# Edge logarithms, first group and first ticks of graph attention beside the projection of linear attention; hidden products and gelu ahead of the gates

## What is computed

```python
xn = _layernorm(x)
x = x + _L0_gnn_ref(xn, ...) + _L0_mix_ref(xn[None], ...)[0]   # GCN + linear attention
x = x + _L0_ffn_ref(_layernorm(x)[None], ...)[0]               # 8 experts of 192, top 2, gelu
xn = _layernorm(x)
x = x + _L1_gnn_ref(xn, ...) + _L1_mix_ref(xn[None], ...)[0]   # graph attention + linear attention
x = x + _L1_ffn_ref(_layernorm(x)[None], ...)[0]               # 8 experts of 3072 + a shared one
```

## Time and profile before

| what | us |
|---|---|
| median of three runs | 2092.32 |
| the profiled execution | 2091.71 |
| its span | 2089.8 |
| TensorE busy in it | 1883.1 |
| VectorE busy | 1306.9 |
| ScalarE busy | 909.6 |
| GpSimd busy | 219.7 |

### The profile page before, as it was taken

How to read it: one execution, slowest core, us unless ns; L and a number is a source line. 1 busy time by engine, 2 the same in 40 slices (tenths; PEclk the granted TensorE clock), 3 DMA queues, 4 the chain that set the end, 5 groups by cost and what they waited for, 6 DMA issues and landing times.

```text
span 2089.8 us, 30875 instructions
## 1 busy us (share of the span) xinstructions
PE 1883.1 (90%) x12246; PEld 1788.8 (86%) x12247; DVE 1306.9 (63%) x2404; ACT 909.6 (44%) x1497; POOL 219.7 (11%) x169
## 2 busy tenths in 40 slices
PE   5988998978997999488757999999999999999998
PEld 4876888977887999488747999999999999999998
DVE  6997766442335544888866575355656666667786
ACT  2331213312222542566733323334555655666776
POOL 0000000003000001565710000000010101000010
PEclk9998999997999999689979999999999999999999
DMA  3110002100111311100022112125565756676895
GB/s 111 46 46 1 24 27 95 54 1 24 69 46 45 106 54 49 64 19 21 16 106 71 53 63 98 69 100 213 190 208 197 234 207 227 245 246 231 284 319 205
DMA packets 36795, 234.29 MB, mean 112 GB/s; under 512 B 5916, under 2 KB 7318, under 8 KB 14632
## 3 DMA queue, kind: packets, MB, share of 16 engines
q1 hardware_dynamic: 31318, 217.41, 29.3%
q0 software_dynamic: 2656, 8.99, 1.9%
q10 hardware_dynamic: 2674, 5.87, 0.7%
HBM read 221.91 MB, written 10.35 MB: 111 GB/s over the span
## 4 chain that ended last, share of the span: by engine, by line
PE 75%; DVE 13%; issue 8%; ACT 2%; DMA 2%; POOL 1%; SPq 0%; DVEq 0%; POOLq 0%; ACTq 0%
PE bank L313 16%; PE bank L315 15%; PE bank L314 15%; PE bank L2441 8%; PE bank L570 4%; PE bank L2442 3%; PE bank L2453 3%; DVE weight_lo L286 2%; PE bank L2457 2%; PE bank L2445 2%; PE bank L2454 2%; PE bank L2456 1%; DVE mix_kv L793 1%; PE bank L2444 1%; DVE gat_unread L2034 1%
## 5 line engine op out<-in xcount | busy, mean ns | idle before, releaser
L286 DVE TENSOR_TENSOR weight_lo<-weight_raw,weight_hi 128x2304 fp32r<-128x2304 f32 (+1 forms) x155 | 389.9, 2519 | 36.7 <-ACT weight_hi L276 36.5
L276 ACT ACTIVATE weight_hi<-weight_raw 128x2304 fp32r<-128x2304 f32 (+1 forms) x155 | 323.3, 2087 | 92.2 <-DMA weight_raw<-in_ffn_w 52.0
L313 PE MATMUL bank<-xT_hi,weight_hi 128*128 128x306 f32 (+1 forms) x576 | 183.8, 319 | 4.0 <-issue 2.0
L314 PE MATMUL bank<-xT_lo,weight_hi 128*128 128x306 f32 (+1 forms) x576 | 178.8, 310 | 0.0
L315 PE MATMUL bank<-xT_hi,weight_lo 128*128 128x306 f32 (+1 forms) x576 | 178.5, 310 | 0.0
L313 PE MATMUL bank<-weight_hi,xT_hi 128*128 128x384 f32 (+1 forms) x480 | 160.2, 334 | 9.3 <-DVE xT_lo L334 4.5
L2815 DVE TENSOR_TENSOR hidden_tmp<-hidden_tmp,bank 128x160 f32<-128x160 f32 (+5 forms) x192 | 65.7, 342 | 160.3 <-ACT hidden_tmp L2601 160.3
L315 PE MATMUL bank<-weight_hi,xT_lo 128*128 128x384 f32 (+1 forms) x480 | 156.8, 327 | 0.0
L314 PE MATMUL bank<-weight_lo,xT_hi 128*128 128x384 f32 (+1 forms) x480 | 156.8, 327 | 0.0
L570 PE MATMUL bank<-one_hot_dst,one_hot_src 125*128 125x313 f16 x800 | 122.8, 305 | 15.2 <-ACT packed_counts L584 7.9
L313 PE MATMUL bank<-weight_hi,hidden_hi 128*128 128x384 f32 (+1 forms) x366 | 124.6, 340 | 0.9 <-DVE weight_lo L286 0.9
(11 more groups left out here) (491 smaller groups left out, 5178.5 us busy)
## 6 DMA issues: line engine op xcount, KB each, us to landing
weight_raw<-in_ffn_w SPq DMA_DIRECT2D x111, 1152.0 KB, 5.2
weight_raw_fifth<-in_ffn_w SPq DMA_DIRECT2D x25, 1152.0 KB, 5.3
weight_raw<-in_shared_w SPq DMA_DIRECT2D x16, 1152.0 KB, 5.2
weight_raw<-in_mix_kv SPq DMA_DIRECT2D x8, 1152.0 KB, 7.1
weight_raw<-in_gat_w SPq DMA_DIRECT2D x8, 768.0 KB, 4.9
weight_raw<-in_mix_q SPq DMA_DIRECT2D x4, 1152.0 KB, 5.1
weight_raw<-in_mix_out SPq DMA_DIRECT2D x4, 1152.0 KB, 5.2
weight_raw<-in_gnn_w SPq DMA_DIRECT2D x4, 1152.0 KB, 5.4
```

The source lines that it names most:

```text
L276: act.activation(upper_, whole_, ACT.Copy).then_inc(*w_hi.one())
L286: dve.tensor_tensor(lower_, whole_, upper_.bitcast(F32), ALU.subtract).then_inc(*w_lo.one())
L313: pe.matmul(dst, a[0], b[0], start=first, stop=False)
L314: pe.matmul(dst, a[0], b[1], start=False, stop=False)
```

## The change

In dense_experts: the logits are made with the gate matrix stationary (8 columns) and 320 tokens moving, 36 matmuls, kept as 8 rows and turned by five transposes. TensorE makes units 0 to 5 of the hidden products around them, then the counts, the gates, unit 6, the seven spread gate rows, and goes on as before from unit 7. gelu goes to `acted`, which holds all units of a half and lies in the place of hT's lower half; the multiply and the lower half are made in place. The weight split that stood behind unit 5 stands ahead of unit 6. The last token tile has 113 columns in the output products, and the pads go.

```diff
+    def logits():
+        pe.wait_ge(*gate_lo.at(1))
+        for s, (a0, n) in enumerate(LOGIT_SPANS):
+            bank = ring.next(logits_kept.at(s + 1))
+            logit_banks.append(bank)
+            product(bank[0:E, 0:n], [(at(gp, ALL, k, ALL), at(xT, ALL, k, slice(a0, a0 + n))) for k in range(KD)]).then_inc(*logits_full.one())
+    def logits_turned():
+        pe.wait_ge(*logits_kept.at(2))
+        bank = ring.next(logits_kept.at(3))
+        logit_banks.append(bank)
+        for t in range(TT):
+            end = pe.transpose(bank[:, t * E:(t + 1) * E], logit_rows[:, tok(t)], ident[0:E, 0:E])
+        end.then_inc(*logits_full.one())
...
+    def hidden(i):
+        hid, _, span, n = unit(i)
+        w = weight("ffn0_w1", i // 6)
+        pe.wait_ge(*xT_ready)
+        bank = ring.next(gelu.at(i + 1))
+        hid_banks.append(bank)
+        mm = hid % 3
+        product(bank[:, 0:n], [(at(w, ALL, k, slice(mm * P, (mm + 1) * P)), at(xT, ALL, k, span)) for k in range(KD)]).then_inc(*hid_full.one())
...
+    hidden(0)
+    hidden(1)
+    logits()
+    hidden(2)
+    logits_turned()
+    hidden(3)
+    hidden(4)
+    hidden(5)
+    counts_turned()
     gates_tensor(gates, gate_banks)
+    hidden(6)
     pe.wait_ge(*gT_lo_made.at(TT))
     pe.wait_ge(*sel_made.at(1))
+    for i in range(EARLY):
+        picked(i)
     for kh in range(2):
...
+        for i in range(max(EARLY, 12 * kh), 12 * (kh + 1)):
+            hidden(i)
+            picked(i)
+        pe.wait_ge(*h_lo.at(12 * (kh + 1)))
         pe.wait_ge(*b2_lo.at(1))
```

ScalarE and VectorE in the same stage:

```diff
+    def hidden(i):
+        hid, k, span, n = unit(i)
+        act.wait_ge(*hid_full.at(i + 1))
+        if i >= 12:
+            act.wait_ge(*y_full.at(2 * TT))
+        act.activation(acted[:, k, span], hid_banks[i][:, 0:n], ACT.Gelu, bias=b1[:, hid:hid + 1]).then_inc(*gelu.one())
+    def hidden_upper(i):
+        _, k, span, _ = unit(i)
+        act.wait_ge(*gated.at(i + 1))
+        upper(at(hT, ALL, k, span), acted[:, k, span]).then_inc(*h_hi.one())
     act.wait_ge(*gate_in.at(16))
     upper(at(gp, ALL, ALL, ALL), gate[:, :, :]).then_inc(*gate_hi.one())
-    logits_scalar(p, logit_banks)
+    act.wait_ge(*b1_in.at(16))
+    hidden(0)
+    hidden(1)
+    for s, (a0, n) in enumerate(LOGIT_SPANS):
+        act.wait_ge(*logits_full.at(s + 1))
+        act.activation(logit_rows[:, a0:a0 + n], logit_banks[s][0:E, 0:n], ACT.Copy).then_inc(*logits_kept.one())
+    hidden(2)
+    act.wait_ge(*logits_full.at(3))
+    act.activation(p[:, :, :], logit_banks[2][:, 0:TT * E].rearrange("p (t e) -> p t e", e=E), ACT.Copy).then_inc(*logits_kept.one())
     act.wait_ge(*soft_low.at(1))
     act.activation(p[:, :, :], p[:, :, :], ACT.Exp).then_inc(*soft_exp.one())
+    hidden(3)
+    act.wait_ge(*sel_filled.at(3))
+    act.activation(sel[:, :, :], sel_f[:, :, :], ACT.Copy).then_inc(*sel_made.one())
+    hidden(4)
+    act.wait_ge(*b2_in.at(16))
+    upper(at(b2p, ALL, ALL), b2[:, :]).then_inc(*b2_hi.one())
+    hidden(5)
     act.wait_ge(*count_f_made.at(TT))
...
         act.wait_ge(*count_turned.at(i + 1))
         act.activation(count[:, t, k0 * P:(k0 + kn) * P], count_banks[i][:, 0:kn * P], ACT.Copy).then_inc(*count_kept.one())
...
+    weights_hi(c0)
+    hidden(6)
+    for i in range(EARLY):
+        hidden_upper(i)
     for kh in range(2):
...
+        for i in range(max(EARLY, 12 * kh), 12 * (kh + 1)):
+            hidden(i)
+            hidden_upper(i)
+            if i % 6 == 5:
+                c = i % 12 // 6
+                weight_read[c0 + 4 * kh + c] = hid_full.at(i + 1)
+                weights_hi(c0 + 4 * kh + c)
...
+    def hidden(i):
+        _, k, span, n = unit(i)
+        dve.wait_ge(*gelu.at(i + 1))
+        dve.wait_ge(*pick_full.at(i + 1))
+        dve.tensor_tensor(acted[:, k, span], acted[:, k, span], pick_banks[i][:, 0:n], ALU.mult).then_inc(*gated.one())
+        dve.wait_ge(*gated.now())
+        dve.wait_ge(*h_hi.at(i + 1))
+        lower(at(hT, ALL, k, span), acted[:, k, span]).then_inc(*h_lo.one())
...
     dve.wait_ge(*b2_hi.at(1))
     lower(at(b2p, ALL, ALL), b2[:, :]).then_inc(*b2_lo.one())
-    dve.memset(tmp[:, 0, :], 0.0).then_inc(*pad_made.one())
-    dve.wait_ge(*pad_hi.at(1))
-    lower(at(hT, ALL, ALL, slice(T + 1, TP)), tmp[:, 0, 0:HK * (TP - T - 1)].rearrange("p (k n) -> p k n", k=HK)).then_inc(*h_lo.one())
...
+        for i in range(12 * kh, 12 * (kh + 1)):
+            hidden(i)
+            if i % 6 == 5 and i > 5:
+                weights_lo(c0 + 4 * kh + i % 12 // 6)
```

```diff
+    weights_load(c0 + 10)
...
     for t in range(TT):
-        if t + 2 < TT:
-            attend(t + 2)
-        project(t, 0)
-        if t + 1 < TT:
-            turn(t + 1)
-        project(t, 1)
+        attend(t)
...
+    weights_hi(c0 + 5)
     per_head(1)
-    weight_read[c0 + 5] = q_full.at(12)
-    turned(0)
-    weights_hi(c0 + 5)
...
     per_head(1)
-    attend(0)
-    attend(1)
-    turned(0)
-    weights_lo(c0 + 5)
     for t in range(TT):
-        if t + 2 < TT:
-            attend(t + 2)
-        project(t, 0)
-        if t + 1 < TT:
...
+for engine in (act, dve, pool, sp):
+    engine.wait_ge(*projection.attended)
...
-        else:
-            sp.wait_ge(*x_ready)
+        sp.wait_ge(*(scored.at(TT * grp) if grp else projection.bias_added))
```

TensorE, ScalarE and VectorE of graph_attention:

```diff
-    for grp, step in FIRST_STEPS:
-        prepare(grp, step)
+    def project(t):
+        projection.project(t, 0)
+        projection.project(t, 1)
+    prepare(0, 0)
+    projection.turn(0)
+    prepare(0, 1)
+    prepare(0, 2)
+    projection.turn(1)
+    prepare(0, 3)
+    prepare(0, 4)
+    projection.project(0, 0)
+    prepare(0, "turned")
+    projection.project(0, 1)
+    projection.turn(2)
+    projection.project(1, 0)
+    prepare(0, "spread")
+    projection.project(1, 1)
+    projection.turn(3)
+    project(2)
+    projection.turn(4)
+    project(3)
+    project(4)
...
+                weight_read[w1_chunk(grp)] = h_full.at(TT * (grp + 1))
+                if grp == 1:
                     weights_hi(c0 - 1)
-                weight_read[w1_chunk(grp)] = h_full.at(TT * (grp + 1))
-                if grp < 3:
+                    weights_hi(c0)
+                if 0 < grp < 3:
                     weights_hi(w1_chunk(grp))
...
+    act.wait_ge(*pick_filled.at(2))
+    act.activation(pick[:, :, :], pick_f, ACT.Copy).then_inc(*pick_made.one())
+    prepare(0, 0)
+    projection.turned_upper(0)
+    prepare(0, 1)
+    prepare(0, 2)
+    projection.turned_upper(1)
+    prepare(0, 3)
+    prepare(0, 4)
+    weights_hi(c0 - 2)
+    act.activation(edge_log[:, :, :], count[:, :, :], ACT.Ln).then_inc(*log_made.one())
+    prepare(0, "turned")
+    projection.turned_upper(2)
+    prepare(0, "spread")
+    act.wait_ge(*b1_in.at(16))
     for i in range(N1 + LAST_LAG + 1):
+        if i == 2:
+            projection.turned_upper(3)
+        if i == 3:
+            projection.turned_upper(4)
+        if i == 5:
+            act.wait_ge(*x_ready)
+            act.dma_start(slots_dram[:, 0:D].rearrange("(t p) d -> p t d", p=P), x[:, :, :]).then_inc(*x_kept.dma())
         q = pair_closing(i, 8)
         if q is not None:
             grp, h, t0, n = pairs_of[q]
...
-            if step == TT - 1 and grp == 0:
+            if step == TT - 1 and grp == 1:
                 weights_lo(c0 - 1)
-            if step == TT - 1 and grp < 3:
+                weights_lo(c0)
+            if step == TT - 1 and 0 < grp < 3:
                 weights_lo(w1_chunk(grp))
...
+    prepare(0, 0)
+    projection.turned_lower(0)
+    prepare(0, 1)
+    prepare(0, 2)
+    projection.turned_lower(1)
+    prepare(0, 3)
+    prepare(0, 4)
+    weights_lo(c0 - 2)
+    prepare(0, "turned")
+    projection.added(0, 0)
+    projection.added(0, 1)
+    projection.turned_lower(2)
     edge_logs()
+    projection.added(1, 0)
+    projection.added(1, 1)
     for i in range(N1 + LAST_LAG + 1):
+        if i == 2:
+            projection.turned_lower(3)
+            projection.added(2, 0)
+        if i == 3:
+            projection.added(2, 1)
+            projection.turned_lower(4)
+            projection.added(3, 0)
+        if i == 4:
+            projection.added(3, 1)
+        if i == 5:
+            projection.added(4, 0)
+            projection.added(4, 1)
         q = pair_closing(i, 8)
         if q is not None:
             grp, h, t0, n = pairs_of[q]
```

More of the change, by code:

```diff
@@ L1 @@
 from contextlib import ExitStack
+from typing import Callable, NamedTuple
 import concourse.bass as bass
@@ L90, in at @@
         return self.semaphore, self.base + n
+class Projection(NamedTuple):
+    attended: tuple
+    bias_added: tuple
+    read: tuple
+    ended: tuple
+    turn: Callable
+    project: Callable
+    turned_upper: Callable
+    turned_lower: Callable
+    added: Callable
 class Ring:
@@ L1218, in tensor @@
                     cols = slice(c * HALF, (c + 1) * HALF)
-                    for t in range(TT):
+                    for t, n in enumerate(ROWS):
```

(14 more changed lines are left out.)

253 lines of the change are left out of this document (92 added, 161 removed).

## The result

The changed kernel takes 2061.53 us (median of 4 runs, 2059.92 to 2062.6) against 2093.32 for the kernel before beside it; the ratio is 0.9844, 95% interval 0.9826 to 0.9861, so 33 us less, 29 to 36. The forecast was 2057.5, range 2046 to 2068. The profiled execution took 2062.6 us, its span is 2060.5, 29.3 less than before. So the total came out 4 us off. That it is so close is in part luck, because two errors stood against each other: in the profiles part A gave 25 us instead of 21, part B 4 instead of 13.5.

The account below looks back on a forecast made before the run. TensorE was taken as the bound, its idle and low-clock time in two stages winnable. Part A 21 us plus part B 13.5 (22.5 less 5.5 and 3.5) made 34.5 us: forecast 2057.5 us, range 2046 to 2068.

Parts of the forecast that it names:

- part A: First experts: logits turned around, hidden products ahead of the gates, gating caught up afterwards; 21 us gained.
- part B: Start of graph attention: all ten half tiles attended first, so its queues open earlier; net 13.5 us gained.
- The twelve units: First experts' gating: seven units at 1.5 us, five at 1.65 us and half a microsecond to enter, ending at 523.2.
- the lock by GpSimd: First experts: GpSimd's five marks on the counts hold up VectorE's split and lower halves; 2 us, ends nothing and 5.3.
- TensorE's own 48.5 us: First experts: units 38.9, logits 5.7 and transposes 3.9 us from xT complete; TensorE through the units at 519.4.
- Rival 2: First experts: GpSimd blocks VectorE for whole instructions, gating falls further behind; 5.3 us instead of 2, 2061 us; chance 0.17.
- The head start of 22.5 us: Graph attention: queues open at 794.5, first edge tile turned at 843.3, tick 5 ends about 844.3 against 866.8.
- Given back to the rows of group 1, 5.5 us: Graph attention: rows behind three weight chunks land 12 to 15 us after x complete; VectorE waits, ends 0 and 8.
- Rival 1: Graph attention: rows of group 1 land in time, making part B 19 us and the total 2052 us; chance 0.17.
- Given back to the splits of tick 8, 3.5 us: Graph attention: two weight splits move from an idle stretch into tick 8, where VectorE is the bound; ends 2 and 5.
- Rival 3: Graph attention: ticks don't start earlier in earnest, VectorE sits on projection sums; part B 4 us, 2067 us; chance 0.12.
- Rival 4: First experts: clock falls at the 8-column stationary logits and stays low until the output products; 2102 us; chance 0.03.

Follow-up runs that it names:

- part_b: Changed kernel with the old dense-experts function of the kernel before, leaving only the new start of graph attention: 2085.55 us, ratio 0.9955 to the kernel before.
- again: The changed kernel unedited, run once more for a second profile: 2060.75 us; its profiled execution took 2053.77 us.
- both: Changed kernel with rows_first's edit and the weight split ahead of the attends moved behind the second half's rows: 2049.31 us, ratio 0.9782 to the kernel before.
- rows_first: Changed kernel with group 1's attention rows issued ahead of three weight chunks, not behind them: 2053.15 us, ratio 0.9815 to the kernel before.
- late_gap: Changed kernel, weight split moved behind the second half's attend rows, three VectorE copies added ahead of mix_att's last lower half: 2063.2 us, one run.

## Why the prediction was right, and where it was not

**What bounds the kernel** held: two poor stages, gains that are separate in time and add (27 and 9 us alone, 33 together: within the intervals of 23 to 31, 6 to 13 and 29 to 36).

**Part A, 21 us forecast, 25 measured.** That the gating chain ends last and that the softmax costs nothing are right. Where the gating starts (503.27 against 503.8) is right on the span only because xT is complete 1.4 us later in this execution (472.17); from there it starts 1.9 us sooner than forecast. Mis-sized were the terms on top. The twelve units were put at 19.4 us and the lock by GpSimd at 2 more; from the first multiply at 503.27 to the start of the output products at 521.79 they take 18.5 with all of it (the two long rows above are 0.3 us each too long, and the first of them lies ahead of the units). The 1 us for a clock that dips behind the gap was not needed in this profile; in five of the ten with this code the clock did fall there, and that cost 1.7 us. With the 0.5 us of the earlier start these make the 4.4 us between 526.2 and 521.79. TensorE's own 48.5 us were right: it runs from 472.27 to 520.07, 47.8, though a stretch that I had not foreseen ran at the low clock (503.1 to 506.5, hence 0.66 over 503 to 508), which the chain covered. The wait of 1.71 instead of 3 to 6 us follows from the shorter chain. Rival 2 is out. The Trainium skill, page SBUF — State Buffer, section SBUF: two separate sides, would have each such pair exclude the other for the whole instruction. The trace does not agree for GpSimd's uint16 marks: the five marks take 2.5 us each, and of the four lower halves beside them three take their usual 0.48 to 0.49 us and one 0.75. With 5.3 us of blocking, as rival 2 put it, part A would have given some 18 us; it gave 25.

**Part B, 13.5 us forecast, 4 measured** (423.4 - 419.5), 3.5 in part_b's profile and 9 between its medians. By its steps:
- *The head start of 22.5 us.* The step that failed is the spacing of the reciprocals: 1.04 us, taken from the kernel before, with the tenth at 792.7 and 1 us more for the split. Counted from the bias add it was forecast at 92.4 us and came at 99.9 (776.17 - 676.28), with 1.92 us between reciprocals. I saw the weight split ahead of the head products, charged it 1 us of time, and did not ask what a pause of TensorE does to its clock. With the clock kept (again) the seventh exponent is 178.7 - 158.7 = 20.0 us early with the row wait in it, and without that wait (both) 26.5. So the head start was under-rated by 4 us; with the low clock 9 of it go at the seventh exponent, and 7 remain lost at the end.
- *Given back to the rows of group 1, 5.5 us.* The mechanism is right, with landing 13.6 us after x complete (forecast 12 to 15) and the idle VectorE ended by the DMA. The size is 9.8. The wait alone was 8.56, above my upper end of 8, since VectorE was there 5.1 us behind x complete and not 7.3; and nothing came back from its later idle spots, where I had taken off 1 to 2 us. Rival 1 is out. The Trainium skill, page DMA: Bandwidth & Descriptors, section Queues, rings and completion order, has the descriptors of a queue consumed in ring order on each DMA engine. rows_first agrees as far as it goes: the same rows ahead of the chunks end the wait.
- *Given back to the splits of tick 8, 3.5 us.* From the seventh to the ninth exponent the kernel before takes 192.3 - 178.7 = 13.6 us, both 169.1 - 152.2 = 16.9: 3.3 us, and moving them wins nothing. Right.
- With these: 26.5 - 3.3 - 2.4 (lost bit by bit to the last sum, cause not sought) = 20.8 for both, measured 423.4 - 402.6; less 9.8 for the rows is 11, measured in again 10.8; less 7 for the clock is 4.
- Rival 3 (the ticks don't start earlier in earnest) predicts 4 us and a time of 2067, and would have looked right by part B's size alone. It is not the cause: with both edits 20.8 of the 26.5 us of head start last.
- Rival 4 had the clock fall in the other stage, at the logits. It did not: 1.00 from 471 to 503. Behind them it fell for 3.4 us only.

**What was to be seen.** Dots near 800 (on the old span, so 775 here; found at 781.3, 773.0 in again), a first turn at 822 to 824 (825.0, and 815.3 in again), a wait for the row, three splits in a row: found. Half clock after 480 was named as what would make part A wrong; it came for 3.4 us at 503, under the chain, and for 20.5 us at 759, in the other part.

**Left open.** Why the clock falls in some executions and not in others of one program; why xT is complete anywhere from 469.9 to 473.1 us; and the 2.4 us above.

## What to carry to other kernels

An edit that makes a dense TensorE stream pause for half a microsecond is not priced by that half microsecond: ask whether the clock survives it, and put splits and copies behind what TensorE waits for, not ahead. The rewritten first experts have such a pause too, of 1.71 us, and pay 1.7 us for it in some executions. Small transfers that are wanted soon go ahead of large ones on their queue, also when the large ones' buffers come free first: here one line gave 9.8 us. And measure stages from a landmark inside the profile, since the total held errors of 4 and 9 us that in part hid each other. Then look at the clock ahead of the landmark as well: here up to 3 us of a spread of 5.5 went with falls of the clock, and the rest came from ahead of the edits.

## What the runs showed of the hardware

- TensorE went from 2.4 to 1.2 GHz at the attends in three of five profiles with a pause of 0.6 us, in two of two with one of 1.4 us, and in none of five without a pause. At the output products of the first experts it did so at 8 of 20 pauses of 1.71 us. In late_gap the matmuls still ran at the high clock for 1.06 us behind the pause (761.72 to 762.78), then at the low one.
- Once down in the attends, the clock stayed at 0.50 for 17 to 20.5 us although TensorE was busy without a pause (759.1 to 779.6 us in the changed kernel). In the output products it came back after 3.4 us.
- In the first experts the clock dipped to 0.50 for 3.4 us between 500.3 and 506.8 us in all ten profiles with the new code, just behind 14 matmuls with 8 stationary rows (500.04 to 502.3 in the changed kernel), and without idle time of TensorE since 472.27. Thirty transposes stand shortly ahead of them (493.75 to 497.19); what brought the dip was not tested.
- GpSimd's uint16 marks beside VectorE's subtractions from two SBUF inputs cost VectorE 0.6 us in 12.4.
